# Moving DVE's weighing of the messages ahead of the logits' sums in a graph-attention kernel

## The reference, cut to what matters

```python
q = (xp @ Wq[l] + bq[l]).reshape(n, H, HD)
k = (xp @ Wk[l] + bk[l]).reshape(n, H, HD)
v = (xp @ Wv[l] + bv[l]).reshape(n, H, HD)
att = jnp.einsum('ehd,ehd->eh', q[dst], k[src]) / scale
att = jnp.nan_to_num(jnp.clip(att, -50.0, 50.0), nan=0.0, posinf=50.0, neginf=-50.0)
...
ex = jnp.exp(att - m[dst])
s = jax.ops.segment_sum(ex, dst, num_segments=n)
alpha = ex / (s[dst] + 1e-16)
msg = (v[src] * alpha[:, :, None]).reshape(-1, D)
aggr = jax.ops.segment_sum(msg, dst, num_segments=n)
x = x + (aggr @ Wo[l] + bo[l])
```

## Time and profile before

| What | Value |
|---|---|
| Median of three runs | 2697.52 us (2687.93 to 2701.51) |
| Span of the profiled execution | 3472.7 us |
| Difference | 775.2 us |
| Mean granted TensorE clock, profiled | 0.807 |
| Busy share PE, DVE, ACT, POOL | 68%, 57%, 49%, 52% |
| First and last gather of the first layer start | 539.4 us, 1947.1 us |
| First and last gather of the second layer start | 2027.2 us, 3411.7 us |

### The profile page before, as it was taken

How to read it: one execution, slowest core, us unless ns; L and a number is a source line. 1 busy time by engine, 2 the same in 40 slices (tenths; PEclk the granted TensorE clock), 3 DMA queues, 4 the chain that set the end, 5 groups by cost and what they waited for, 6 DMA issues and landing times.

```text
span 3472.7 us, 60241 instructions
## 1 busy us (share of the span) xinstructions
PE 2377.0 (68%) x13853; PEld 2027.0 (58%) x13854; DVE 1981.1 (57%) x7060; ACT 1704.5 (49%) x4472; POOL 1820.8 (52%) x1968
## 2 busy tenths in 40 slices
PE   6998774567667676777667746666666666666667
PEld 6988333556556565656556635556565565565556
DVE  7887782455555555555556625555555455554555
ACT  6765653345445444545445434354444445454444
POOL 5642655655555555555555245556555555555552
PEclk9999885778878878878888867788778778787788
DMA  7865232222322222222223122222222222222221
GB/s 211 242 207 172 88 106 85 85 77 84 89 86 84 84 79 85 79 86 82 82 83 88 45 72 83 82 81 84 81 77 78 81 79 81 77 81 81 78 84 37
DMA packets 180176, 323.48 MB, mean 93 GB/s; under 512 B 38740, under 2 KB 93991, under 8 KB 179892
## 3 DMA queue, kind: packets, MB, share of 16 engines
q0 software_dynamic: 80208, 216.22, 21.7%
q1 hardware_dynamic: 98948, 103.44, 9.7%
q10 hardware_dynamic: 736, 0.93, 0.1%
HBM read 288.09 MB, written 20.71 MB: 89 GB/s over the span
## 4 chain that ended last, share of the span: by engine, by line
another core or an unknown queue 15%; PE 13%; issue 10%; DVE 8%; DVEq 3%; ACT 3%; ACTq 0%; DMA 0%; SPq 0%
PE bank L2080 5%; DVE aggregate L2120 3%; PE bank L2071 2%; PE bank L1729 2%; PE bank L1723 1%; DVE arena L2128 1%; ACT arena L2013 1%; PE bank L2056 1%; PE bank L1720 1%; DVE arena L2148 1%; DVEq L2109 1%; DVE arena L2162 1%; DVEq L2120 1%; PE bank L1718 1%
## 5 line engine op out<-in xcount | busy, mean ns | idle before, releaser
L1992 POOL DMA_INDIRECT arena<-kv_rows,idx_stage x1612 | 1540.8, 956 | 1344.6 <-DVE arena L2128 798.4
L2080 PE MATMUL bank<-arena 128*128 128x136 f32 x3328 | 698.7, 359 | 654.1 <-DVE aggregate L2120 551.8
L2120 DVE TENSOR_TENSOR aggregate<-bank,aggregate 128x136 f32 x1664 | 493.9, 297 | 1017.6 <-remote 851.3
L2080 PEld LDWEIGHTS bank<-arena 128*128 128x128 f32 x3328 | 589.1, 249 | 746.1 <-DVE aggregate L2120 419.9
L2071 PE MATMUL bank<-queries,arena 128*128 x3328 | 547.5, 317 | 82.0 <-DVE arena L2148 53.6
L2071 PEld LDWEIGHTS bank<-queries,arena 128*128 128x128 f32 x3328 | 509.9, 233 | 91.3 <-issue 90.8
L2013 ACT ACTIVATE arena<-iota_n,at_negdst 128x128 f32<-128x128 f32 x1664 | 527.7, 395 | 3.8 <-DMA kv_rows<-arena 2.0
L1777 ACT ACTIVATE arena<-bank 128x256 f32<-128x256 f32 (+1 forms) x225 | 85.0, 379 | 731.8 <-remote 454.8
L2056 PE MATMUL bank<-ident,arena 128*128 128x128 f32 x1664 | 325.7, 329 | 106.1 <-issue 63.0
L2148 DVE TENSOR_TENSOR arena<-bank,arena 128x512 f32<-128x512 f32 x416 | 284.6, 684 | 152.8 <-remote 68.2
L2037 ACT ACTIVATE arena<-arena 128x32 f32<-128x32 f32 x416 | 92.8, 223 | 556.0 <-DVE arena L2177 336.3
(11 more groups left out here) (322 smaller groups left out, 2796.3 us busy)
## 6 DMA issues: line engine op xcount, KB each, us to landing
arena<-in_edge_attr_dram SPq DMA_DIRECT2D x244, 256.0 KB
arena<-kv_rows,idx_stage POOLq DMA_INDIRECT x1612
kv_rows<-arena SPq DMA_DIRECT2D x12, 512.0 KB, 3.8
kv_rows<-arena SPq DMA_DIRECT2D x24, 256.0 KB, 2.2
arena<-in_x_dram SPq DMA_DIRECT2D x12, 256.0 KB, 4.0
x_rows<-arena SPq DMA_DIRECT2D x12, 256.0 KB, 2.9
x_stream<-arena SPq DMA_DIRECT2D x12, 256.0 KB, 2.3
queries<-arena SPq DMA_DIRECT2D x12, 256.0 KB, 2.7
```

The lines of the kernel that those rows point to most:

```text
L1992: pool.indirect_dma_start(kv[:, n, :], None, kv_dram[l], bass.IndirectOffsetOnAxis(idx_stage[:, half % 2, n:n + 1], 0)).then_inc(Z.kv_in[s ...
L2080: pe.matmul(sums_of(j), sel[:, r % SEL_SLOTS, j, :], msg[:, r % 2, j, :], start=True, stop=True).then_inc(Z.sum, 1)
L2120: dve.tensor_tensor(a, sums_of(j), a, ALU.add).then_inc(Z.added, 1)
```

## The change

In DVE's quad, `weigh` moves from behind the sum per head to right behind the product (and behind the register load of even quads), and `join(0)` moves from there to behind the sum per head. No instruction is added, removed or changed in size; waits keep their values. The other engines' code is the same.

```diff
                     def join(j):
                         if not (first and r < 2):
                             add(k - 2, j, tiles[r % 2 * QUAD + j])
-                    join(0)
+                    if not (first and r == 0):
+                        weigh(k - 1, (r - 1) % QUADS)
                     update(i, r, 1)
                     dve.wait_ge(Z.prod, k0 + k + 1)
                     dve.tensor_reduce(a[:, 0, :], prod[:, r % 2, :, :].rearrange("p j (h c) -> p (j h) c", h=HEADS), AX_X,
                                       ALU.add).then_inc(Z.att, 1)
                     update(i, r, 2)
-                    if not (first and r == 0):
-                        weigh(k - 1, (r - 1) % QUADS)
+                    join(0)
                     update(i, r, 3)
                     join(1)
                     update(i, r, 4)
```

## The result

The changed kernel takes 2720.79 us (median of five runs, 2713.25 to 2728.18) against 2698.13: a ratio of 1.0092, 95% interval 1.0074 to 1.0110. It is 0.9% slower. A second job gave 2727.51 against 2696.87, 1.0113 (1.0083 to 1.0142). The time lies in the predicted range, but the forecast was "no change", and the change costs 23 us.

The account below looks back on a forecast made before the run. It took POOL's gather issue, 2645 to 2693 us of the 2697.5 median, as the bound; DVE's +85 + 50 - 92 - 35 = +8 us, or -193 with stops, was mostly hidden, so -1 us gave 2696, range 2620 to 2740.

Parts of the forecast that it names:

- the sum for POOL alone: POOL's span with its waits taken out, 1.25 us per gather in both layers: 2693.0 us, against a median of 2697.5.
- upper end: The most that POOL alone should take, 2693.0 us; 2645 if DVE's last product followed the last gather sooner.
- 5 to 53 us: Part of the median run left for quads in which POOL is held up.
- sign of error: Runs moving by over 14 us would mean POOL's issue isn't the bound outside the profile.
- (a): DVE's addition 1 directly follows addition 0 and waits for it: +0.30 us in 283 quads, 85 us of DVE time.
- (b): DVE's messages ask earlier for ACT's exponentials: 50 us more waiting where DVE bounds, nothing where POOL bounds.
- (c): DVE's addition 0 asks 1.19 us later for PE's sums: -92 and -35 us, plus 201 of unnamed stops filled.
- (d): DVE writes messages 0.80 us earlier, so POOL may refill slots sooner; no gain expected from the eight-quad ring.
- where POOL bounds it is hidden: DVE's changed time, +8 us or -193 with stops, disappears behind its spare 0.9 us per quad.
- the stops: Long idle times of DVE and ACT, about 6 to 7 us in the example, read as mostly belonging to the profiled execution.
- span near 3300: The changed kernel's profiled span, perhaps down to 3300 us as additions' waits fall by 100 to 250, runs not following.
- slower rival: Adjacent additions delay PE's sums, PE having 0.14 us per quad to spare: 39 to 85 us, 2736 to 2782; chance 0.13.

Follow-up runs that it names:

- second profile: The kernel before, unedited, profiled again in a job without long stops: 2697.06 us, span 2695.0.
- added product: The kernel before plus one unused 128x512 DVE product of two SBUF inputs per quad, ahead of addition 3: 0.9999 in the 3.5 ms condition, 1.0215 in the 2.7.
- added sum per head: The kernel before plus one unused 0.68 us one-input DVE sum per quad, ahead of addition 3: 3497.99 us, 1.0066, in the 3.5 ms condition.
- Order b: The kernel before with DVE reordered to product, messages, addition 0, logits' sums, addition 1: 2725.32 us, 1.0095, in the 2.7 ms condition.
- Order a: The kernel before with DVE reordered to product, sums, addition 0, messages, addition 1: 2689.24 us, 0.9967; in the 3.5 ms condition 3436.33, 0.9721.
- order d: The kernel before with DVE reordered to product, logits' sums, messages, additions 0 and 1: 3606.6 us, then 3575.63 (1.0291), both in the 3.5 ms condition.
- messages in halves: The kernel before with messages made in two halves of two steps, addition 1 between: 2672.73 us, 0.9909; in the 3.5 ms condition 3512.45, 1.0099.

## Why the prediction was right and wrong

**Right: what bounds the kernel, though the sum met the median by luck.** POOL's chain of gathers sets the time of the runs. Done again with the second profile's times (first gather at 543.3, 53.2 at the turn of the layers, 36.3 behind the last gather), the sum for POOL alone is 543.3 + 1007.5 + 53.2 + 1007.5 + 36.3 = 2647.8. The span is 2695.0, so 47.2 us are missing, and the excess of the gathers is 47.2. The prediction's upper end, 2693.0, had the long ends of the 3.5 ms condition in it (27.6 us from the last gather to DVE's last product, here 5.7) in place of the long gathers. It put the "5 to 53 us" down to quads in which POOL is held up; they are gathers that last longer. Its own sign of error misled, too: the runs moved by 23 us, more than the 14 it named, and POOL's issue is the bound all the same.

**Right: (a) and (b) as costs of DVE, hidden.** In the changed kernel 312 additions directly follow another one, and most begin 0.43 to 0.51 us after it, 0.48 on the mean, instead of 0.21. That is 84 us of DVE's time (5 in the kernel before, from 14 such pairs), against 85 expected: more pairs than the 283 counted, each a little cheaper than 0.30. The 17 us that the prediction worked out from the Trainium skill's 60 ns are far too few here. The wait for exponentials rose from 15.0 to 79.4 us, against the 29 to 79 of the sum. For the POOL-bound state the prediction had said that the exponentials are ready by then and the item is nothing; that was wrong for the wait, right for the time. Neither is paid. (c), the wait of additions for PE, fell from 14.2 to 3.1 us and "issue" from 52.8 to 6.0: won, and likewise worth nothing. (d), POOL asking earlier, had nothing to win.

**Wrong: "where POOL bounds it is hidden".** This step of the sum took the gather's 1.25 us for a constant. I had read that its record "hardly varies" from a median in the earlier trace rows whose maximum, 1432 and 1527, stands in the same row. The moved operation lies beside the gathers, and its place decides how many it holds and for how long: +25.8 us. The cover of a hidden operation must be free of it; here the cover was the bound, and the two share something. The Trainium skill names a candidate, page "SBUF — State Buffer", section "SBUF: two separate sides": DVE and GpSimd share a port pair under an exclusive lock, which a DVE operation with two SBUF inputs takes too, though only against a GpSimd operation that reads SBUF, and whichever starts first blocks the other for the whole instruction. (A gather here does take its row numbers from `idx_stage`, a tile in SBUF.) The traces agree on one side: messages and added product (two inputs in SBUF) hold gathers to 0.82 us behind their end, while the added sum per head (one input, 279 gathers at 0.945 us) and the product of queries and keys (one input in PSUM, 136 gathers beginning in it in the changed kernel, 0.945 on the mean) don't. On the other side they differ, and the measurement decides: messages that begin within 0.03 us behind a gather take 0.695 to 0.724 us instead of 0.68 to 0.69, and those that begin 0.3 to 0.6 us behind one take their usual time. A gather doesn't block DVE for its whole 0.946 us. That the hold comes from this port, and not from something else that two inputs need, no run here shows.

**Wrong: the stops.** They were not the profile's doing. The rule that the prediction took from the Trainium skill, page "NOTIFIC — the notification-queue block", section "7.1 Overflow: three behaviours, one of which stalls the engine", doesn't explain a condition in which the runs without a profile take 3.5 ms as well. The forecast of a span near 3300 failed with it: the changed kernel takes 3551 there, 2.0% more. The additions' unnamed waits did fall, from 839 to 565 us, more than the 201 that item (c) counted, and nothing of it reached the time.

**Wrong: the slower rival's mechanism.** It was given 0.13, through the adjacent additions and PE. The slower time came by neither. Order b, without adjacency, is as slow. The range reached up to 2740 for this rival's sake, so that 2720.79 lies in it is luck.

## What stays open

What makes the 3.5 ms condition isn't known, nor why the order costs more there. Order a wins 2.8% in it, in one job. Its sums, which need nothing of PE's latest work, go ahead of the addition that is stopped; that this is the reason was expected for its repeat, which came in the other condition, and is not shown. The early messages lose there, in b and in the changed kernel, and so does order d with late messages and adjacent additions (2.9% in the second job); neither is explained. Messages are written earlier, and POOL waits 851 to 903 us for them all the same. Order d wasn't timed in the 2.7 ms condition, nor the one-input operation, whose effect on gathers is read from traces alone, nor order a with messages in halves, which the two gains suggest.

One of the 22 executions of the kernel before in the job of the added operations took 10096.51 us; nothing here explains it, and the median doesn't move with it.

Order a is faster than the kernel before in both conditions, 0.3% and 2.8%. Messages in halves win 0.9% in the first and lose 1.0% in the second.

## What to carry to other kernels

When POOL's indirect DMAs bound a kernel, a DVE operation with two float32 inputs in SBUF can cost time, however much DVE has to spare: 0.68 us of it held a gather by up to 0.6 us. Make such operations short, or place them by the timeline between the beginnings of two gathers. And take a duration's maximum and sum, not its median, before calling an operation constant; before explaining away a profile that doesn't match the runs, get a second one.

## What the runs showed of the hardware beyond expectation

A gather that begins while DVE runs a product of two SBUF inputs, and would end less than 0.82 us after the product, ends 0.82 us after it, in all three kinds of such products looked at (128x512 messages, 128x512 added product, 128x256 of the node update). A sum with one input of the same 0.68 us leaves it at 0.945. The same program takes 2.70 ms in one job and 3.47 to 3.53 in another, with a mean granted TensorE clock of 0.93 to 0.94 and 0.80 to 0.81; each job holds its condition, and one chip gave both.
